# First attention: maxima subtracted by GpSimd before the turning, and the dot product multiplied twice from PSUM

## The reference

```
q, k, v: 16 heads of 16 columns, from x @ w_qkv + b_qkv
dot    = q . k
scores = dot * dot / (|q|^2 + |k|^2 - 2 * dot + 1e-6) + causal mask of -1e9
out    = softmax(scores) @ v, then @ w_out + b_out
```

## Time and profile before

| | us |
|---|---|
| median of three runs | 3496.45 (3488.12 to 3507.61) |
| profiled execution, its own time | 3478.68 |
| its span | 3476.5 |
| first attention, first Ln to last product | 73 to 1482 |
| busy in the span: TensorE, VectorE, ScalarE, GpSimd | 3129.8, 2289.0, 1984.5, 875.5 |

### The profile page before, as it was taken

How to read it: one execution, slowest core, us unless ns; L and a number is a source line. 1 busy time by engine, 2 the same in 40 slices (tenths; PEclk the granted TensorE clock), 3 DMA queues, 4 the chain that set the end, 5 groups by cost and what they waited for, 6 DMA issues and landing times. The chain is left out here.

```text
span 3476.5 us, 78108 instructions
## 1 busy us (share of the span) xinstructions
PE 3129.8 (90%) x29924; PEld 2203.4 (63%) x29924; DVE 2289.0 (66%) x6197; ACT 1984.5 (57%) x3528; POOL 875.5 (25%) x1874
## 2 busy tenths in 40 slices
PE   3999999999999999988996888888888889799999
PEld 1677777777777777732333666766676667566666
DVE  2888888888888888844224666666666666333333
ACT  1888888888888888822331444444444445222222
POOL 0222222222222222216111222322222222233222
PEclk9999999999999999988997999999999999999999
DMA  5333333333333333210003443434343433000000
GB/s 152 60 56 58 58 58 58 58 59 58 58 58 58 55 55 56 39 41 0 0 0 69 79 76 61 80 61 80 64 76 64 77 63 51 1 19 19 19 19 25
DMA packets 109267, 182.65 MB, mean 53 GB/s; under 512 B 26336, under 2 KB 95712, under 8 KB 96416
## 3 DMA queue, kind: packets, MB, share of 16 engines
q1 hardware_dynamic: 105440, 176.87, 27.7%
q10 hardware_dynamic: 3456, 0.79, 0.2%
HBM read 116.51 MB, written 60.29 MB: 51 GB/s over the span
## 5 line engine op out<-in xcount | busy, mean ns | idle before, releaser
L1207 DVE TENSOR_REDUCE zeroed_max_cols<-bank 128x1 f32<-128x512 f32 (+3 forms) x1024 | 450.2, 481 | 251.6 <-PE bank L180 249.7
L1107 ACT ACTIVATE zeroed_prob<-bank 128x512 f32<-128x512 f32 x640 | 377.6, 597 | 326.6 <-PE bank L998 244.3
L636 DVE CUSTOM_DVE_ANT_0 ratio_scores<-ratio_scores 128x512 f32<-128x512 f32 (+3 forms) x1024 | 521.7, 537 | 22.1
L177 PE MATMUL bank<-ratio_k_stack,ratio_q_stack 102*128 102x512 bf16 (+7 forms) x2048 | 453.4, 303 | 66.4 <-ACT ratio_inv_root L506 46.4
L506 ACT ACTIVATE ratio_inv_root<-bank,eps_ratio 128x512 f32<-128x512 f32 x640 | 437.5, 684 | 111.6 <-PE bank L180 107.8
L627 DVE TENSOR_TENSOR ratio_scores<-bank,ratio_inv_root 128x512 f32<-128x512 f32 x640 | 437.8, 684 | 62.1 <-PE bank L177 54.9
L425 PE MATMUL bank<-const_f_sb,ratio_scores 128*128 128x128 f32 x2560 | 451.5, 274 | 1.1 <-ACT ratio_prob L515 0.4
L508 ACT ACTIVATE ratio_inv_root<-ratio_inv_root 128x512 f32<-128x512 f32 x640 | 404.0, 631 | 20.3
L180 PE MATMUL bank<-const_b_sb 128*128 128x128 bf16 x2048 | 393.4, 224 | 0.0
L515 ACT ACTIVATE ratio_prob<-bank 128x512 f32<-128x512 f32 x640 | 370.5, 579 | 6.0 <-PE bank L431 5.8
L425 PEld LDWEIGHTS bank<-const_f_sb,ratio_scores 128*128 128x128 f32 x2560 | 301.3, 141 | 59.1 <-DVE ratio_max_cols L636 2.2
(11 more groups left out here) (176 smaller groups left out, 5613.9 us busy)
## 6 DMA issues: line engine op xcount, KB each, us to landing
ratio_q_stack<-ratio_parts_q SPq DMA_DIRECT2D x192, 128.0 KB
ratio_k_stack<-ratio_parts_k SPq DMA_DIRECT2D x192, 128.0 KB
zeroed_q_stack<-zeroed_parts_q SPq DMA_DIRECT2D x192, 128.0 KB, 4.6
zeroed_k_stack<-zeroed_parts_k SPq DMA_DIRECT2D x192, 128.0 KB, 7.2
ratio_parts_q<-ratio_parts SPq DMA_DIRECT2D x96, 128.0 KB
ratio_parts_k<-ratio_parts SPq DMA_DIRECT2D x96, 128.0 KB
zeroed_parts_q<-zeroed_parts SPq DMA_DIRECT2D x96, 128.0 KB
zeroed_parts_k<-zeroed_parts SPq DMA_DIRECT2D x96, 128.0 KB
```

The source lines that it names most:

```text
L177: i = e.matmul(bank[:, off:off + w], qs[0:rows, s, hh, ib * P:(ib + 1) * P], ks[0:rows, s, hh, 0:w], start=(k == 0), stop=mask is None, sk ...
L636: i = e.tensor_tensor_reduce(seg, seg, seg, 1.0, 0.0, ALU.mult, ALU.max, mx[:, pair % M_BUFS, c:c + 1])
L1107: e.activation(prob[:, n % FOLD_PROBS, 0:wd], exp_banks[n % 2][:, 0:wd], ACT.Exp, scale=0.25).then_inc(s["prob"])
L1207: i = e.tensor_reduce(mx[:, pair % FOLDS, c:c + 1], bank[:, off:off + (ib + 1) * P], AX_X, ALU.max)
```

## The change

GpSimd subtracts the maxima itself: after the reduce of unit n it takes each block of scores less the block's maximum, one column spread over the block's width (`less`). With that `split_maxima`, `turn_maxima`, `keep_maxima`, the selecting constants and the matmul L428 are gone. The inverse is now 1/denominator (Exp with scale -1), and VectorE multiplies twice by the dot product: once in `weigh`, once in the reduce `maxima`, which now reads the dot bank in PSUM as well as the scores in SBUF. So a dot bank is free only after the reduce. The copy of a group's result out of PSUM goes from VectorE to ScalarE. The bias of Ln is given as a number and not as a column of SBUF. The lag of the turning goes from 10 units to 6, the row's steps from (57, 60, 62, 64) to (53, 55, 57, 59), the score buffers from 11 to 9 and the sets of maxima from 5 to 3.

```diff
-BACK_LAG = 10
+BACK_LAG = 6
-S_BUFS, INV_BUFS, PROB_BUFS = 11, 3, 13
-M_BUFS = 5
+S_BUFS, INV_BUFS, PROB_BUFS = 9, 3, 13
+M_BUFS = 3
+EPS_RATIO = 1.0e-6
-RATIO_GROUP, RATIO_ROW = BACK_LAG + N_UNITS + 5, (57, 60, 62, 64)
+RATIO_GROUP, RATIO_ROW = BACK_LAG + N_UNITS + 5, (53, 55, 57, 59)
 def dots(n):                                          # TensorE
-    q.wait_ge(s["ratio"], n - 1)
+    q.wait_ge(s["maxima"], n - 1)
-def shift(n):
+def turn(n):
-    q.wait_ge(s["maxima"], n + 1)
-    q.wait_ge(s["post_read"], post["maxima", pair])
+    q.wait_ge(s["lessened"], n + 1)
-        e.matmul(bank[:, off:off + wd], net.cb[:, B_PICK + c * P:B_PICK + (c + 1) * P],
-                 mT[:, pair % M_BUFS, :].unsqueeze(1).to_broadcast([P, ib + 1, P]),
-                 start=False, stop=False, skip_group_check=True)
 def inverse(n):                                       # ScalarE
-    e.activation(to, den_bank[:, 0:wd], ACT.Ln, scale=-2.0, bias=net.eps_ratio[:, :]).then_inc(s["log_den"])
+    e.activation(to, den_bank[:, 0:wd], ACT.Ln, scale=-2.0, bias=EPS_RATIO).then_inc(s["log_den"])
-    e.activation(to, to, ACT.Exp, scale=-0.5).then_inc(s["inv_root"])
+    e.activation(to, to, ACT.Exp, scale=-1.0).then_inc(s["inverse"])
+def keep_group(g):                                    # ScalarE, from VectorE
+    e.activation(o_group[:, :], o_bank[:, :], ACT.Copy).then_inc(s["o_group"])
 def maxima(n):                                        # VectorE
-    q.wait_ge(s["m_neg"], pair - M_BUFS + 1)
+    q.wait_ge(s["lessened"], (pair + 1 - M_BUFS) * PAIR_UNITS)
-        i = e.tensor_tensor_reduce(seg, seg, seg, 1.0, 0.0, ALU.mult, ALU.max, mx[:, pair % M_BUFS, c:c + 1])
+        i = e.tensor_tensor_reduce(seg, dot_banks[n % 2][:, at], seg, 1.0, 0.0, ALU.mult, ALU.max,
+                                   mx[:, pair % M_BUFS, c:c + 1])
+def less(n):                                          # GpSimd
+    q.wait_ge(s["maxima"], n + 1)
+    for h, ib, off in UNITS[n % N_UNITS]:
+        w, c = (ib + 1) * P, m_col(h, ib)
+        seg = scores[:, n % S_BUFS, off:off + w]
+        i = e.tensor_tensor(seg, seg, mx[:, pair % M_BUFS, c:c + 1].to_broadcast([P, w]), ALU.subtract)
+    i.then_inc(s["lessened"])
...
```

More of the change, by code:

```diff
@@ L45, in constants @@
     b[:, B_EXP1:B_EXP1 + P] = MASK_DROP * (row >= col)
-    for s in range(8):
-        for part in range(3):
-            b[part * 8 + s, B_PICK + s * P:B_PICK + (s + 1) * P] = 1.0
     return f, b
@@ L196, in attend @@
     return i
[L199 to L211, removed]
 class AttentionWeights:
@@ L410, in dots @@
                 q.wait_ge(*gathered(n // HALF_UNITS))
-                q.wait_ge(s["ratio"], n - 1)
+                q.wait_ge(s["maxima"], n - 1)
                 product(e, net, n, dot_banks[n % 2], qs, ks, STACK, None).then_inc(s["dots"])
-            def shift(n):
-                g, u = divmod(n, N_UNITS)
-                pair, bank = n // PAIR_UNITS, exp_banks[n % 2]
-                q.wait_ge(s["maxima"], n + 1)
-                q.wait_ge(s["post_read"], post["maxima", pair])
+            def turn(n):
+                bank = exp_banks[n % 2]
+                q.wait_ge(s["lessened"], n + 1)
                 q.wait_ge(s["prob"], n - 1)
                 first = True
-                for h, ib, off in UNITS[u]:
-                    wd, c = (ib + 1) * P, m_col(h, ib)
+                for _, ib, off in UNITS[n % N_UNITS]:
+                    wd = (ib + 1) * P
                     for jb in range(ib + 1):
@@ L479, in pe @@
                 if 0 <= n - BACK_LAG < total:
-                    shift(n - BACK_LAG)
-                if n % PAIR_UNITS == TURN_SLOT and 0 < n // PAIR_UNITS <= total // PAIR_UNITS:
-                    turn_maxima(n // PAIR_UNITS - 1)
+                    turn(n - BACK_LAG)
                 if half + 1 < halves:
@@ L575, in act @@
                     keep_row(b, step // 2)
+                g, part = divmod(n - BACK_LAG - N_UNITS, N_UNITS)
+                if 0 <= g < total // N_UNITS and part == len(ATTEND):
+                    keep_group(g)
         def dve(q):
@@ L707, in dve @@
                         net.row_stats(q, b, net.stats_out, s["out_stats"], s["out_aggr"])
-                g, part = divmod(n - BACK_LAG - N_UNITS, N_UNITS)
-                if 0 <= g < total // N_UNITS and part == len(ATTEND) - 1:
-                    keep_group(g)
         def pool(q):
@@ L755, in pool @@
                 half, at = divmod(n, HALF_UNITS)
-                pair, i = divmod(n, PAIR_UNITS)
-                if i == 1 and 0 < pair <= total // PAIR_UNITS:
-                    split_maxima(pair - 1)
+                if n < total:
+                    less(n)
                 if half + 1 < halves:
```

83 lines of the change are left out of this document (23 added, 60 removed).

## The result

| | before | after |
|---|---|---|
| median of seven runs each, us | 3490.18 (3487.03 to 3507.61) | 3526.55 (3513.63 to 3533.81) |
| profiled execution, us (its span) | 3478.68 (3476.5) | 3529.36 (3527.6) |
| first attention, up to its end, us | 1509.8 | 1534.3 |
| low-rank, second attention, last stage, us | 331.3, 1150.1, 485.3 | 322.3, 1185.6, 485.3 |

The changed kernel is slower: ratio 1.0085 from all seven runs of each, with a 95% interval of 1.0061 to 1.0109 (the two medians alone give 1.0104). The forecast was 3462 in a range of 3388 to 3522, with 0.61 on faster. One execution of 9788 us, among the twelve of the run with the next row's statistics at 18, is in no ratio.

What follows compares the result with a forecast made beforehand. The slower of TensorE and ScalarE, sharing one denominator bank, was taken to set each iteration. Schedule -38, dot banks +6, late gather +3 and drain -5 gave -34 us: 3462 against the median 3496.45, range 3388 to 3522.

Steps and rivals of the forecast that it cites:

- Lag and row steps: First attention: attends, turning and row steps move; larger engine per iteration sums to 86.4 us a round, -2.4 x 16 = -38.
- the drain: End of the first attention: six units instead of ten trail the last product, -5 us in all.
- The sum that was said to hold: First attention before the change: larger of TensorE and ScalarE over 40 iterations, 88.8 us against 88.1 measured.
- +6 for the dot banks: First attention: dot banks are freed by the reduce, not the first product; 0.4 us a round charged, +6 us.
- +3 for a late gather: First attention: TensorE waits for a gather that lands late, +0.2 x 16 = +3 us.
- Ln's bias: ScalarE's Ln (L506): a number instead of a column takes 0.10 us off each of 640, floor 1.62 us.
- Rival 5: ScalarE's Ln: the number is still a column, the floor stays 1.72 us; 3491 us, chance 0.08.
- The reduce: VectorE's L636: 0.69 us instead of 0.780 on average, no extra for PSUM; with such excesses -2.9 us a round.
- Rival 3: First attention: GpSimd becomes the bound if its subtraction takes half more; +110 us, 3606, chance 0.07.
- Rival 2: First attention: VectorE's casts wait for GpSimd; at 90 us a round +19, 3515 us, chance 0.13.
- Rival 1: First attention: engines give way to each other between neighbouring iterations; at 82 us a round -109, 3387 us, chance 0.17.
- Rival 4: First attention: the DMA gather sets the half, each of 32 waits 1 us more; gain gone, 3494 us, chance 0.06.

Runs made afterwards that it cites:

- the candidate: Changed kernel with lag 10, row steps 57, 59, 60, 67 and the next row's statistics at step 18: ratio 0.9862 to the kernel before, round 86.01 us.

## Why the prediction was wrong, by its steps

The median of 3526.55 lies 5 us above the range, but the miss is larger than that: for the stage it is -34 forecast and +24.5 measured. What the medians differ by beyond that (36 us in all) belongs to stages that were not edited, as told above.

- **Lag and row steps: the step that failed.** It set each iteration to the larger of TensorE and ScalarE and gave 86.4. With VectorE's two statistics outside iterations 19 and 20, and all else as in the change, the round is 87.29; with them there it is 91.25, and the stage is 58 us longer (1534.3 against 1476.0). That is the term at nothing in the sum: -34 + 58 = +24. With the statistics apart the stage is 33.8 shorter than before, nearly the forecast's 34, and that nearness is partly luck: from the first Ln to the last 24.1 us went where the sum had 38 - 6 - 3 = 29, the first Ln came 3.0 earlier, which the sum did not have, and the drain gave 6.8 for 5. The term was left out in two places: the table had no column for VectorE, and ScalarE's root stood in it with its own 0.63 though it waits for VectorE's statistics. I took VectorE by its average (73 of 86 us) and did not ask where in the round its work lies. My own sentence on the moved steps named attends and turning, and not the final sum and the statistics that move with step 59 onto VectorE.
- **The sum that was said to hold** did so by its total: 88.8 for a measured round of 88.87. Of its iterations before the change, 26 was 3.12 and measured 3.93, 24 was 4.85 and measured 4.40, and 0, 10 and 30 were 0.34 too long. A sum that is checked by its total alone hides what it leaves out.
- The +6 for the dot banks and +3 for a late gather were too high: the weight loads wait 4.1 us in all for the reduce, and the gather's 10.9 us of the earlier trace rows are 2.3. The drain was right (-5, measured -6.7).
- **Ln's bias:** right, 593 ns; light iterations 1.63 to 1.65 for 1.62. Rival 5 is out. Its price of 3491 leaves out the sum's own +6 and +3; with them it is 3499.
- **The reduce:** right, 692 ns, none of the excess of the earlier trace rows left. The Trainium skill's rule (VectorE: DVE Perf Modes, "The TRN2 errata") of 120 fixed cycles for a PSUM source and 58 for SBUF does not show: 692 from PSUM and SBUF, 0.69 from SBUF alone.
- **GpSimd:** 864 of 1438 us, 60% where I expected 75%, since it takes 1048 ns and not 1265 for 512 columns. Rival 3 is out.
- **Rival 2**, the loss side: right in its sign and wrong as the cause. The normalisation was held: L559 went from 408 to 717 ns, 60 x 0.309 = 18.5 us of VectorE in all. It has the same 717 ns in the kernels with the old lag (0.9874), of the candidate (0.9862) and with the statistics apart (0.990), and they are faster than before. The casts L571 took 427 ns as before, but that says nothing for them: none of the 64 began while a GpSimd instruction ran. With the old lag 31 of them did, and took 490 ns in the mean, as did 31 of the norms' casts at 554 instead of 419. So casts are held as well, by 0.06 to 0.14 us each, far from the 1.27 of the worst case.
- **Rival 1** is out: no iteration falls below ScalarE's 1.62, and the round is far from 82. Four iterations (6, 15, 26, 35) are 0.3 to 0.5 below the sum, and the two behind 6 and 26 are 0.2 above it, so a little is made up or was priced too high; which of the two stays open.
- **Rival 4** is out for the changed kernel, whose gather wait is 2.3 us. With the old lag it came true in kind: 1.8 us in each of 31 halves.
- **What would show it:** I named casts, the wait in front of the products and turning as signs of failure. The sign that came, the root's wait for the statistics, was a row of 17.6 us that I had passed over.

## What to carry to other kernels

When a step of a hand-written pipeline is moved, list its instructions on every engine, and lay each engine's queue out iteration by iteration, the one with the lowest average too: here 1.8 us of VectorE in front of another 1.8 us lengthened one iteration by 3.65 us, in 14 of 16 rows. In the sum, a cross-engine wait gets the time at which its releaser can be done, not the waiting instruction's own length. And test a way of computing apart from the schedule that comes with it: the same arithmetic was 1.3% faster with the old schedule and 0.85% slower with the new.

## What the runs showed of the hardware

- A reduce with one input in PSUM and one in SBUF ran beside GpSimd's two-input subtraction at 692 ns; with both in SBUF it took 830 on average, and GpSimd's own instruction grew from 614 to 812 ns.
- A tensor-scalar of 128x256 fp32 with two column operands is held by GpSimd: in the changed kernel 30 of 64 began while a GpSimd instruction ran and took 1024 ns in the mean, the others 409. A cast from fp32 to bf16 is held as well, but by less: in the kernel with the old lag, one that began while a GpSimd instruction ran took 490 ns for 128x512 and 554 for 64x512, and one that did not 426 and 420.
- GpSimd's subtraction of one spread column took 1048 ns for 512 columns; a sum with two full inputs takes 1265.
- After TensorE idled 4.09 us it came back at a granted clock of 0.75 of full over the next 6.7 us. The second attention, which nobody edited, took 1185.6 and 1154.9 us in two executions of the changed kernel, with 240 and 161 us of it at 1.2 GHz.
